# Local attention on five engines: the parts of each half step take another order on ScalarE, TensorE, VectorE and GpSimd

## The reference, cut to what matters

```
q, k, v = split(x @ Wqkv)                       # 16 heads of 64
q = l2norm(q) * q_scale ;  k = l2norm(k) * k_scale
q = q * cos * scale + rotate_half(q) * sin * scale
k = k * cos / scale + rotate_half(k) * sin / scale
sim  = q_window @ k_two_windows.T * 8 ;  sim = where(mask, -max, sim)
out  = softmax(sim) @ v_two_windows
x    = x + out @ Wo
```

## Time and profile before

| | before |
|---|---|
| median of 3 runs | 3875.07 us (3874.39 to 3875.17) |
| the profiled execution's own time | 3872.81 us |
| its span, first to last instruction | 3871.0 us |
| mean granted TensorE clock | 0.971 |
| busy in the span: TensorE, its weight loads | 3542.8 us (92%), 2679.4 us (69%) |
| busy: VectorE, ScalarE, GpSimd | 2948.5 us (76%), 3021.4 us (78%), 2494.8 us (64%) |

### The profile page before, as it was taken

One profiled execution on the slowest core, in us unless ns is written; L12 is line 12 of the kernel. 1 busy time (PEld: TensorE's weight loads), 2 busy tenths in 40 slices (PEclk: granted clock), 3 DMA queues, 4 the chain that ended last, 5 costly groups with the idle time before them and its releaser, 6 DMA issues.

```text
span 3871.0 us, 95171 instructions
## 1 busy us (share of the span) xinstructions
PE 3542.8 (92%) x30888; PEld 2679.4 (69%) x30894; DVE 2948.5 (76%) x4344; ACT 3021.4 (78%) x6096; POOL 2494.8 (64%) x2313
## 2 busy tenths in 40 slices
PE   5898679999889999889999899999799999799998
PEld 3444357777567777577777577776577777577776
DVE  4666378886788886788886788886788886788876
ACT  3556478887688887688887698886688886788885
POOL 3555377775377774577773577773677772677762
PEclk8999799999999999999999899999899999899999
DMA  4223200000100000000001000001000001000002
GB/s 134 86 91 94 55 2 1 0 0 1 30 2 0 0 0 22 9 2 0 0 0 30 2 2 0 0 0 30 2 1 0 0 1 29 2 1 0 0 1 72
DMA packets 59745, 67.76 MB, mean 18 GB/s; under 512 B 12006, under 2 KB 40164, under 8 KB 58468
## 3 DMA queue, kind: packets, MB, share of 16 engines
q1 hardware_dynamic: 59492, 64.64, 5.8%
HBM read 46.27 MB, written 18.35 MB: 17 GB/s over the span
## 4 chain that ended last, share of the span: by engine, by line
ACT 37%; issue 25%; PE 21%; DVE 12%; ACTq 2%; POOL 2%; DMA 1%; SPq 0%; DVEq 0%; POOLq 0%
PE bank L401 18%; ACT sb_area L790 18%; ACT bank L790 5%; DVE sb_area L1280 4%; ACT sb_area L940 4%; DVE sb_smax L1277 4%; ACT sb_lnb L952 3%; ACT sb_lnb L949 3%; ACT sb_area L983 2%; PE bank L673 1%; DVE sb_area L1155 1%; DVE sb_area L1257 1%; PE bank L614 1%; DVE sb_ssq L1267 1%; DMA sb_wqk_lo<-qk_rows 1%
## 5 line engine op out<-in xcount | busy, mean ns | idle before, releaser
L790 ACT ACTIVATE sb_area<-bank 128x512 f32<-128x512 f32 (+4 forms) x2149 | 1335.2, 648 | 209.4 <-PE bank L401 154.9
L1257 DVE TENSOR_TENSOR sb_area<-bank,sb_rots 128x1024 f32<-128x1024 f32 x768 | 939.1, 1225 | 393.7 <-ACT sb_area L940 392.9
L1520 POOL TENSOR_TENSOR sb_area<-sb_area,sb_rn 128x512 f32<-128x512 f32 x768 | 785.7, 1044 | 586.3 <-ACT sb_rn L956 586.3
L401 PE MATMUL bank<-sb_area 128*64 128x64 f32 (+6 forms) x17104 | 1062.2, 275 | 21.2 <-ACT bank L790 8.7
L1506 POOL TENSOR_TENSOR sb_area<-sb_area 128x512 f32<-128x512 f32 x768 | 969.4, 1280 | 86.6 <-DVE sb_area L1257 84.8
L401 PEld LDWEIGHTS bank<-sb_area 128*64 128x64 f32 (+4 forms) x17104 | 746.9, 145 | 283.1 <-issue 229.5
L401 PE MATMUL bank<-sb_wqk_hi,sb_xwin 128*128 128x512 f32 x1536 | 723.6, 473 | 55.7 <-DVE sb_xwin L1237 47.6
L401 PE MATMUL bank<-sb_area,sb_wvo 128*128 128x256 f32 x3072 | 728.3, 381 | 3.1 <-DVE sb_xT L1312 3.1
L401 PEld LDWEIGHTS bank<-sb_area,sb_wvo 128*128 128x128 f32 x3072 | 555.0, 190 | 78.4 <-issue 12.8
L614 PE MATMUL bank<-sb_ident,sb_area 128*128 128x128 f32 x3072 | 488.4, 282 | 39.9 <-ACT sb_area L790 31.2
L614 PEld LDWEIGHTS bank<-sb_ident,sb_area 128*128 128x128 f32 x3072 | 354.6, 143 | 235.6 <-issue 124.8
(11 more groups left out here) (115 smaller groups left out, 3979.4 us busy)
## 6 DMA issues: line engine op xcount, KB each, us to landing
qk_rows<-sb_p SPq DMA_DIRECT2D x52, 256.0 KB, 4.2
sb_wqk_hi<-qk_rows SPq DMA_DIRECT2D x32, 256.0 KB, 2.9
sb_wqk_lo<-qk_rows SPq DMA_DIRECT2D x32, 256.0 KB, 2.7
sb_area<-in_Wqkv SPq DMA_DIRECT2D x7, 1024.0 KB, 6.1
sb_area<-in_WvT SPq DMA_DIRECT2D x7, 512.0 KB, 7.4
sb_wo_bd<-in_Wo SPq DMA_DIRECT2D x14, 256.0 KB, 8.3
sb_area<-in_x SPq DMA_DIRECT2D x4, 512.0 KB, 6.1
sb_area<-in_x SPq DMA_DIRECT2D x8, 256.0 KB, 2.9
```

Source lines behind the costliest of these rows:

```text
L401: return nc.tensor.matmul(o, a, b, start=start, stop=stop, skip_group_check=True)
L790: return nc.scalar.activation(o, i, ACT.Copy)
L1257: tt_(t12[:, c % 2, :, :].rearrange("p u (h d) -> p u h d", h=8), src, bc(rots[:, tt, s, :, :], [P, 2, 8, D], 2), ALU.mult).then_inc(S["ro ...
L1520: pt_(qn[:, c, :].rearrange("p (h d) -> p h d", h=8), qsum[:, c % 2, :].rearrange("p (h d) -> p h d", h=8), r, ALU.mult).then_inc(S["qn"], 1)
```

## The change

ScalarE: a half begins with the mask for this half's scores, which now waits for the subtraction (`sub`) of the half before; then the first copy from `rbank`, both squares, the exponential of the half before (it stood at the end of its own half), the norms of the half before, `turned_p`, `weighed`, in the second half the window copy (before: in the first), in the first half `heads_of_tokens`, and the second copy from `rbank`. TensorE: `turn_qk(2wp)` comes first, then both projections, `turn_p`, `weigh` ahead of `score`, the windows in the second half (before: the first), so that `turn_qk(3)` is the one that waits for `xwev`. VectorE: `sums` after both rotations. GpSimd: `add(2wp)` first and `add(2wp+1)` last, with the scales and `normalise` between; the add writes `qn` directly and waits for the transposes (`tr`) of that slice, and the scale works on `qn` in place; `qsum` is gone. The buffer of squares grows from two slices to four.

```diff
@@ -147,8 +147,8 @@
             return v.rearrange(f"p ({names}) -> p {names}", **dict(zip("abcde", shape)))
 
         ysb = take(2, 8, HEADS * WIN)
-        sqb, t12 = take(2, 512), take(2, 2, 512)
-        qsum, qn = take(2, 512), take(4, 512)
+        sqb, t12 = take(4, 512), take(2, 2, 512)
+        qn = take(4, 512)
         dd, pT = take(2, 512), take(2, 512)
         xw = take(TT, 2, C)
 
@@ -606,7 +606,7 @@
                         g = g_of(bt) * 16 + (4 * tt + c)
                         pe.wait_ge(S["qn"], g + 7)
 
-                        if c == 1:
+                        if c == 3:
                             pe.wait_ge(S["xwev"], g_of(bt) * 4 + tt + 1)
                         else:
                             pe.wait_ge(S["ev"], g)
@@ -668,7 +668,7 @@
                             return
                         tt, bt = v
                         g = g_of(bt) * 4 + tt
-                        pe.wait_ge(S["ev"], g * 4 + 1)
+                        pe.wait_ge(S["ev"], g * 4 + 3)
                         for wp in range(2):
                             m = nc.tensor.transpose(rbank[:, wp * P:(wp + 1) * P], xs[:, tt * P + wp * WIN:(tt + 1) * P + wp * WIN],
                                                     ident[:, :])
@@ -700,14 +700,14 @@
                         for b in range(4):
                             mean(b)
                     for wp in range(2):
+                        turn_qk(2 * wp)
                         project(2 * wp)
-                        turn_qk(2 * wp)
+                        project(2 * wp + 1)
                         turn_p(wp)
-                        project(2 * wp + 1)
+                        weigh(4 - wp, 1 - wp)
                         score(wp)
-                        if wp == 0:
+                        if wp == 1:
                             windows()
-                        weigh(4 - wp, 1 - wp)
                         turn_qk(2 * wp + 1)
                         project_out(wp)
                     join_weights()
@@ -936,16 +936,16 @@
                         tt, bt = v
                         g = g_of(bt) * 16 + (4 * tt + c)
                         act.wait_ge(S["proj"], g + 1)
-                        act.wait_ge(S["ssq_raw"], g)
-                        nc.scalar.activation(sqb[:, c % 2, :], pj[c % 2][:, :], ACT.Square).then_inc(S["sq"], 1)
-
-                    def norms(half):
-
-                        if not (v := behind(t, i, part, 0)):
+                        act.wait_ge(S["ssq_raw"], g + 1 - c % 2)
+                        nc.scalar.activation(sqb[:, c, :], pj[c % 2][:, :], ACT.Square).then_inc(S["sq"], 1)
+
+                    def norms(lag, half):
+
+                        if not (v := behind(t, i, part, lag)):
                             return
                         tt, bt = v
                         n = (g_of(bt) * 4 + tt) * 2 + half
-                        act.wait_ge(S["ssq_raw"], 2 * n + 3)
+                        act.wait_ge(S["ssq_raw"], 2 * n + 5)
                         nc.scalar.activation(lnb[:, tt % 2, half, :], ssq[:, tt % 2, half, :], ACT.Relu,
                                              bias=guard[:, 0:1]).then_inc(S["ssq"], 1)
                         act.wait_ge(S["ssq"], n + 1)
@@ -975,17 +975,19 @@
                                      rbank[:, :].rearrange("p (j q) -> p j q", j=4))
                         m.then_inc(S["ev"], 1)
 
-                    def exp(wp):
-                        if not (v := behind(t, i, part, 2)):
+                    def exp(lag, wp):
+                        if not (v := behind(t, i, part, lag)):
                             return
                         tt, bt = v
                         act.wait_ge(S["sub"], g_of(bt) * 8 + 2 * tt + wp + 1)
                         nc.scalar.activation(dd[:, wp, :], dd[:, wp, :], ACT.Exp).then_inc(S["exp"], 1)
 
-                    def mask_ahead(wp):
-                        if not (v := behind(t, i, part, 2)):
-                            return
-                        first = v[0] == TT - 1 and wp == 1
+                    def mask_ahead(lag, wp):
+                        if not (v := behind(t, i, part, lag)):
+                            return
+                        tt, bt = v
+                        act.wait_ge(S["sub"], g_of(bt) * 8 + 2 * tt + wp + 1)
+                        first = tt == TT - 1 and wp == 1
                         copy(sbank[:, :], lmask[:, 0 if first else 1, :]).then_inc(S["masked"], 1)
 
                     def turned_p(wp):
@@ -1018,19 +1020,19 @@
                         copy(xw[:, tt, :, :], rbank[:, 0:256].rearrange("p (w c) -> p w c", w=2)).then_inc(S["xwev"], 1)
 
                     for wp in range(2):
+                        mask_ahead(3 - wp, 1 - wp)
+                        turned_qk(2 * wp)
                         square(2 * wp)
-                        turned_qk(2 * wp)
+                        square(2 * wp + 1)
+                        exp(3 - wp, 1 - wp)
+                        norms(1 - wp, 1 - wp)
                         turned_p(wp)
-                        square(2 * wp + 1)
-                        if wp == 0:
+                        weighed(4 - wp, 1 - wp)
+                        if wp == 1:
                             windows()
-                            if not (part == 0 and t == 0) and (v := behind(t, i, part, -1)):
-                                heads_of_tokens(*v)
-                        weighed(4 - wp, 1 - wp)
+                        elif not (part == 0 and t == 0) and (v := behind(t, i, part, -1)):
+                            heads_of_tokens(*v)
                         turned_qk(2 * wp + 1)
-                        exp(wp)
-                        mask_ahead(wp)
-                        norms(wp)
                     joined_weights()
                     if part == 2 and t == LAG + 2 * TT - 1:
                         for b in range(4):
@@ -1107,7 +1109,7 @@
             nc.vector.memset(guard[:, 0:1], -1e-24)
             nc.vector.memset(guard[:, 1:2], 1e-24).then_inc(S["guard_set"], 1)
             column = iter(range(28))
-            for name, n in (("sq", 1), ("rotd", 1), ("ssq_raw", 1), ("add", 1), ("tr", 3), ("score", 2), ("yy", 2),
+            for name, n in (("sq", 1), ("rotd", 1), ("ssq_raw", 3), ("add", 1), ("tr", 3), ("score", 2), ("yy", 2),
                             ("pt", 2), ("qn", 6), ("ln_part", 3), ("pn", 1), ("oo", 1)):
                 for _ in range(n):
                     c = next(column)
@@ -1264,7 +1266,7 @@
                         g = g_of(bt) * 16 + (4 * tt + 2 * half)
                         dve.wait_ge(S["sq"], g + 3)
                         dve.wait_ge(S["ln_part"], g_of(bt) * 8 + 2 * tt + half)
-                        nc.vector.tensor_reduce(ssq[:, tt % 2, half, :], sqb.rearrange("p c (h d) -> p (c h) d", h=8), AX.X, ALU.add)\
+                        nc.vector.tensor_reduce(ssq[:, tt % 2, half, :], sqb[:, 2 * half:2 * half + 2, :].rearrange("p c (h d) -> p (c h) d", h=8), AX.X, ALU.add)\
                             .then_inc(S["ssq_raw"], 2)
 
                     def shift(wp):
@@ -1319,9 +1321,9 @@
                         for b in range(4):
                             deviation(b)
                     for wp in range(2):
-                        sums(3 - wp, 1 - wp)
                         rotate(2 * wp)
                         rotate(2 * wp + 1)
+                        sums(3 - wp, 1 - wp)
                         shift(wp)
                         square_sums(wp)
                         if wp == 0:
@@ -1500,10 +1502,10 @@
                             return
                         tt, bt = v
                         g = g_of(bt) * 16 + (4 * tt + c)
-                        pool.wait_ge(S["qn"], g + 5)
+                        pool.wait_ge(S["tr"], g)
                         pool.wait_ge(S["rotd"], g + 2)
                         swapped = t12[:, c % 2, 1, :].rearrange("p (h e d) -> p h e d", h=8, e=2)[:, :, ::-1, :]
-                        pt_(qsum[:, c % 2, :].rearrange("p (h e d) -> p h e d", h=8, e=2),
+                        pt_(qn[:, c, :].rearrange("p (h e d) -> p h e d", h=8, e=2),
                             t12[:, c % 2, 0, :].rearrange("p (h e d) -> p h e d", h=8, e=2), swapped, ALU.add)\
                             .then_inc(S["add"], 1)
 
@@ -1515,10 +1517,9 @@
                         half = c // 2
                         pool.wait_ge(S["rn"], g_of(bt) * 8 + (2 * tt + half + 1))
                         pool.wait_ge(S["add"], g + 2)
-                        pool.wait_ge(S["tr"], g)
                         r = rn[:, tt % 2, half, 8 * (c % 2):8 * (c % 2) + 8].unsqueeze(2).to_broadcast([P, 8, D])
-                        pt_(qn[:, c, :].rearrange("p (h d) -> p h d", h=8),
-                            qsum[:, c % 2, :].rearrange("p (h d) -> p h d", h=8), r, ALU.mult).then_inc(S["qn"], 1)
+                        sums_of_heads = qn[:, c, :].rearrange("p (h d) -> p h d", h=8)
```

(4 more changed lines are left out.)

## The result

The changed kernel takes 4041.64 us (median of 4 runs, 4040.14 to 4045.90): 1.0434 [1.0416, 1.0452] of the kernel before, 167 us more than the 3874.73 us measured beside it. The profiled execution took 4040.95 us, its span is 4038.8 us, the mean granted clock 0.969 (before 0.971).

The account below looks back on a forecast made before the run. Half A was taken as bound by ScalarE, half B by TensorE. The profiled 3872.8 us, +173 for steps and -18 for layer starts, gave 4028, forecast as 4030 us; 3960 to 4130 was to hold 8 in 10.

Parts of the forecast that it names:

- The step: One tile of 128 tokens, in two halves: 15.29 us against 14.22, +1.07, over 162 full steps +173 us.
- Half B: Second half of a step (`wp` 1): 8.03 us, with TensorE idle about 0.95 us waiting for the window copy.
- T2: Second four-transpose group of a half, `turn_qk(2wp+1)`; in Half B to start at 5.84 us, after the window copy.
- Half A: First half of a step (`wp` 0): 7.26 us, with TensorE idle about 0.5 us waiting for the odd query copy.
- the heads: ScalarE's `heads_of_tokens` between weighed and the odd query copy in Half A, priced at 0.37 us.
- T1: First four-transpose group of a half, `turn_qk(2wp)`; results 0.60 us after its start, 0.10 more until ScalarE can copy.
- The start of a layer: First five steps: ScalarE's wait before norms goes, 3 us saved a layer, -18 in all, ends 0 and -36.
- DVE's 0.2 us: Cover at ScalarE's mask: VectorE's subtraction may come 0.2 us later at no cost; beyond that, one for one.
- POOL's cover: GpSimd's first scale was to end 1.1 us before the transposes that need it, costing nothing.
- rival (3): Clock falls to 0.93: +60 us for TensorE's work on the path, 170 if all grew; about 4090 to 4200; chance 0.07.
- Rival (1): TensorE alone binds, halves 6.75 and 7.11, step 13.86 us: faster, 3799 us; chance 0.09.
- Rival (4): GpSimd's second add, now behind T2, comes late and holds rotations and projections: 162 us more, 4192; chance 0.04.

Follow-up runs that it names:

- project_first: The changed kernel with TensorE projecting before the first transposes of each half and ScalarE squaring before it copies, windows still in the shared bank: 3945.76 us.
- the first experiment: The changed kernel with GpSimd's second scale of a half moved behind normalise, nothing else touched: 4044.30 us.
- windows_own_bank: The changed kernel with the window transposes put into `tbank`, the bank of the attention weights, instead of `rbank`: 3855.04 us.
- both_sums_first: The changed kernel with windows in `tbank`, the exponential right behind the mask, and VectorE's sums and reciprocal ahead of the rotations: 3901.55 us.
- own_bank_project_first: The changed kernel with windows in `tbank` and a projection ahead of the first transposes of each half: 3753.66 us.

## Why the prediction was right or wrong

**Sign and size** were right: 4030 us forecast, 4041.64 measured, by the forecast's own mechanism. Two terms were off in opposite directions, the steps by 16 us too much and the starts by 31 too little, so that the forecast came within 12 us is in part luck.

**The step.** +1.07 was predicted, +0.97 measured (mean of the six layers). Half B was right to the hundredth: 8.03 against 8.04; T2 at 5.84 after T1, measured 1913.70 - 1907.85 = 5.85; the gap on PE 0.95, marked 0.86. Half A was 7.11 and not 7.26. Its stall is 7.11 - 6.74 (half A of project_first) = 0.37, not 0.5; the marked 0.22 is less, since the record of `project_out` in front (1.89 us) runs past where the next group can start (1915.89 - 1914.17 = 1.72). The term that was off is the heads, taken at 0.37 from the earlier trace rows, where ACT's next copy also waited for weighing: that ends at 1823.17 + 1.13 = 1824.30, and the copy starts at 1824.38. Here the odd copy follows after 1906.52 - 1906.32 = 0.20. The rest was within 0.1 (T1's results 0.64 after its start and not 0.70, the way back 0.15 and not 0.05). So 162 x 0.97 = 157 us in place of 173.

**The start of a layer** is the step that failed. "Half a step later that wait is gone", -3 us a layer, was forecast; the first five steps grew by 2.2, so about +13 us in six layers instead of -18, outside the bounds of 0 and -36. (157 + 13 is 170, 167 were measured: the first layer began at 485.1 us instead of 487.9.) The wait did go: ACT waited 7.2 us for the sums of squares ahead of its norms in the first five steps of one layer of before,

```profile
ACT sb_lnb L949 <- DVE sb_ssq L1267: 7.2, 3, 3.1
```

and never there in after, where one wait of 0.8 us ahead of a square is left. But I had counted T1's place at the head of PE's queue in the steady step only. The waits of PE in the first five steps of one layer (total us, times, longest us), of after and of project_first:

```profile
PE bank L614 <- POOL sb_area L1522: 10.0, 5, 2.7
PE bank L614 <- ACT sb_area L790: 7.3, 6, 2.6
```

```profile
PE bank L614 <- ACT sb_area L790: 6.5, 5, 1.8
PE bank L614 <- POOL sb_area L1522: 4.9, 5, 1.3
```

Where stages are missing, PE reaches T1 before the scale or the copy is done, and the projections that could fill that time stand behind it: 17.3 us of waiting, against 11.4 with a projection in front. These 5.9 us are also what the first five steps differ by (67.0 and 61.1). With the projection first, the starts do fall, by 3.7 us a layer below before (61.1 against 64.8): the predicted gain is there, and T1's new place eats it.

**Covers.** DVE's 0.2 us held: in the steady stretch ACT's mask waits for the subtraction once, for 0.2 us. POOL's cover held as well, though the page names POOL; "T1 released by POOL's scale" was listed as a sign against the forecast, and would have misled. **The clock** stayed at 1.00 in the steady stretch, with PE idle for 28 of 390 us, so rival (3) did not occur. (Its upper price was a little low: at 0.93 a whole step of 15.29 grows by 1.15 us, 186 us in 162 steps, not 170.) The Trainium skill, "TensorE: Matmul & The Clock Gate", section "A second HAM failure mode: psum-queue depth-cycling", tells of a kernel in which frequent small idle times between groups of matmuls made the clock swing; this trace, with two such gaps a step and a granted clock of 1.00, does not show it. **Rival (1)**, PE alone, is what the kernel does once both hand-overs are gone: PE's own halves were put at 6.75 and 7.11 and are 6.73 and 6.98. **Rival (4)** fell with the first experiment as far as POOL's order goes; the in-place add itself was not undone.

**Which part costs what.** The window copy in front of T2: about 186 us (after against windows_own_bank), 150 when added to before alone. T1 ahead of the projection: 96 us alone, 101 with the windows out of the way. Together they cost 288 us; without them the rest of the change gains some 120 us on before.

## What to carry to other kernels

When two engines share one bank, look for the work that each can do between giving it up and needing it again: a transpose with nothing behind it but the next user of the same bank costs the whole way there and back, here 0.4 to 1.5 us, however short the copy. Before believing a releaser's name or the chain of waits, see whether another event ends within some 0.1 us of it, and move one of the two. A change that loses can hold a gain: after two edits this one is 3.0% faster than before.

## What the runs showed of the hardware that was not expected

Small DVE instructions between SBUF tensors last much longer when GpSimd works beside them. Of before (first three lines) they ran while POOL waited for the norms; of after, timelines of DVE and POOL:

```profile
L1237 DVE TENSOR_TENSOR sb_xwin<-sb_xs,sb_xwin 128x128 fp32r<-128x128 f32 x24 | 6.8, 281 | 0.0
L1230 DVE COPY sb_xs<-sb_xT 64x128 f32 (+1 forms) x24 | 5.4, 225 | 0.3
L1229 DVE COPY sb_xs<-sb_xT 64x128 f32 x24 | 5.0, 209 | 0.0
```

```profile
1915.39 1.35 DVE L1231 COPY sb_xs<-sb_xT 64x128 f32 x1
1916.76 0.23 DVE L1232 COPY sb_xs<-sb_xT 64x128 f32 x1
```

```profile
1915.40 1.26 POOL L1508 TENSOR_TENSOR sb_area<-sb_area 128x512 f32<-128x512 f32 x1
```

The first copy ends with POOL's add (1916.74 and 1916.66), and takes 1.35 us; the next, with POOL idle, takes 0.23. This is no single case: in 300 us of the steady loop of after 34 of these small instructions took over 0.4 us, and each of them ended 0.08 to 0.15 us behind an instruction of POOL; in before, where none of 61 ran beside POOL, the longest took 0.28. Rotations, which read one operand from PSUM, did not change (1225 ns before, 1217 after). The Trainium skill, "SBUF — State Buffer", section "SBUF: two separate sides", says that a VectorE instruction in a two-port mode, as fp32 copies within SBUF are, or with two SBUF inputs beside a GpSimd one that reads SBUF, takes turns with GpSimd's at a shared pair of ports, a whole instruction at a time; the trace agrees, with the ends just given. In after this costs next to nothing, since DVE has time to spare; in both_sums_first, with DVE full, it takes up to 2.3 us of each step. That it alone keeps that kernel from 13.7 us was not tried: own_bank_project_first steps in 13.74 us with DVE busy for 98 of 100.
